# Rotary attention in a six-layer stage: each score step writes two single PSUM banks, and its exponential is done in two halves

## The reference, cut to what matters

```python
def _attn(q, k, v, mask):
    scores = jnp.einsum('bqhd,bkhd->bhqk', q, k) / np.float32(np.sqrt(HD))
    scores = jnp.where(mask[:, None, None, :], jnp.float32(-jnp.inf), scores)
    w = jax.nn.softmax(scores, axis=-1)
    return jnp.einsum('bhqk,bkhd->bqhd', w, v)
...
for i in range(NL):
    xn = _adaln(x, noise_emb, n1_w[i], n1_b[i])
    ...
    q = _rope(q.reshape(B, L, H, HD))
    k = _rope(k.reshape(B, L, H, HD))
    a = _attn(q, k, v, src_mask).reshape(B, L, D) @ so_w[i].T
    x = x + a
    ...
    a = _attn(q, k, v, ctx_mask).reshape(B, L, D) @ co_w[i].T
    x = x + a
    xn = _adaln(x, noise_emb, n3_w[i], n3_b[i])
    h = jax.nn.gelu(xn @ f1_w[i].T + f1_b[i], approximate=False)
    x = x + (h @ f2_w[i].T + f2_b[i])
```

## Time and profile before

| | |
|---|---|
| median of 3 runs | 4170.21 us (4165.55 to 4171.18) |
| the profiled execution | 4145.95 us, span of its instructions 4144.1 us |
| busy: TensorE, VectorE, ScalarE, GpSimd | 3599.2, 2465.0, 2296.2, 1355.3 us |
| stage 6 | from about 2269 us to the end, some 1875 us |
| mean granted TensorE clock | 0.949 of full speed |

### The profile page before, as it was taken

One profiled execution on the slowest core, in us unless ns is written; L12 is line 12 of the kernel. 1 busy time (PEld: TensorE's weight loads), 2 busy tenths in 40 slices (PEclk: granted clock), 3 DMA queues, 4 the chain that ended last, 5 costly groups with the idle time before them and its releaser, 6 DMA issues.

```text
span 4144.1 us, 56756 instructions
## 1 busy us (share of the span) xinstructions
PE 3599.2 (87%) x22327; PEld 1596.7 (39%) x22327; DVE 2465.0 (59%) x4758; ACT 2296.2 (55%) x3200; POOL 1355.3 (33%) x1355
## 2 busy tenths in 40 slices
PE   5699999899568988998895889898999998988886
PEld 4477433333443344334552233233333332333333
DVE  6732444544225345543658877777778677777754
ACT  4543554454124554545321766777767676776683
POOL 5500233333224511441003234344343442433411
PEclk8699999999799999999896999999999999999998
DMA  2000000000330010001111101111111110110100
GB/s 118 1 21 1 31 16 22 6 16 22 128 109 11 17 32 27 16 17 56 39 27 44 36 25 38 52 27 45 43 32 40 43 47 25 43 47 25 41 12 16
DMA packets 126956, 146.41 MB, mean 35 GB/s; under 512 B 36141, under 2 KB 107637, under 8 KB 124866
## 3 DMA queue, kind: packets, MB, share of 16 engines
q1 hardware_dynamic: 125664, 140.67, 11.5%
q0 software_dynamic: 1024, 2.10, 0.2%
HBM read 74.63 MB, written 6.43 MB: 20 GB/s over the span
## 4 chain that ended last, share of the span: by engine, by line
PE 59%; DVE 22%; ACT 8%; POOL 5%; DMA 3%; issue 3%; SPq 1%; POOLq 0%; DVEq 0%; ACTq 0%
PE ps L1903 6%; PE ps L1919 6%; PE ps L2114 6%; DVE c1sm L2862 4%; DVE c0sm L2862 4%; PE ps L2031 3%; PE ps L1823 3%; PE ps L1815 3%; PE ps L2100 3%; ACT wB L2358 2%; PE ps L2058 2%; PE ps L1951 2%; PE ps L1844 2%; PE ps L2158 2%; POOL c1m L3043 2%
## 5 line engine op out<-in xcount | busy, mean ns | idle before, releaser
L2358 ACT ACTIVATE wB<-ps 128x1024 f32<-128x1024 f32 (+1 forms) x762 | 762.1, 1022 | 270.0 <-PE ps L2100 263.8
L2862 DVE TENSOR_REDUCE c1sm<-ps 128x2 f32<-128x1024 f32 x384 | 456.6, 1220 | 128.1 <-PE ps L2058 125.3
L2862 DVE TENSOR_REDUCE c0sm<-ps 128x2 f32<-128x1024 f32 x384 | 453.2, 1219 | 97.2 <-PE ps L2058 95.3
L2656 DVE TENSOR_REDUCE c1sm<-ps 128x2 f32<-128x1024 f32 x128 | 151.7, 1220 | 194.0 <-PE ps L1868 192.8
L2656 DVE TENSOR_REDUCE c0sm<-ps 128x2 f32<-128x1024 f32 x128 | 152.5, 1221 | 172.3 <-PE ps L1868 171.3
L2358 ACT ACTIVATE c0m<-ps 128x1024 f32<-128x1024 f32 (+1 forms) x198 | 202.4, 1022 | 70.0 <-PE ps L2100 68.0
L2114 PE MATMUL ps<-wB,c1m 128*18 128x512 f32 (+1 forms) x1216 | 205.5, 611 | 1.1 <-DVE c1sm L2869 0.6
L1903 PE MATMUL ps<-c0ar 64*128 64x512 f32 (+1 forms) x640 | 178.1, 634 | 20.8 <-DVE c0sm L2656 9.1
L2100 PE MATMUL ps<-c0ar 64*128 64x512 bf16 (+1 forms) x864 | 167.0, 388 | 33.0 <-DVE c1sm L2862 14.4
L2100 PE MATMUL ps<-c1ar 64*128 64x512 bf16 (+1 forms) x864 | 165.3, 392 | 26.5 <-DVE c0sm L2862 9.2
L2992 POOL TENSOR_SCALAR c0sm<-c0sm 128x4 f32<-128x4 f32 x40 | 7.8, 194 | 547.9 <-DVE c0sm L2430 462.5
(11 more groups left out here) (918 smaller groups left out, 8268.1 us busy)
## 6 DMA issues: line engine op xcount, KB each, us to landing
c0ar<-c0m SPq DMA_DIRECT2D x216, 128.0 KB, 2.4
c1ar<-c0m SPq DMA_DIRECT2D x216, 128.0 KB, 2.4
c0m<-rscr SPq DMA_DIRECT2D x96, 128.0 KB, 2.9
c1m<-rscr SPq DMA_DIRECT2D x96, 128.0 KB
wA<-in_lay SPq DMA_DIRECT2D x6, 1346.0 KB, 5.6
c0ar<-in_x SPq DMA_DIRECT2D x15, 512.0 KB, 3.5
c1ar<-in_x SPq DMA_DIRECT2D x15, 512.0 KB
wA<-in_w SPq DMA_DIRECT2D x1, 4248.0 KB, 22.0
```

The source lines that it names most:

```text
L2358: e.activation(P.ap[0:n, :, :], u.ap[0:n, :].rearrange("p (a q) -> p a q", a=2), ACT.Exp, scale=S8).then_inc(*A(("P8", n0, s, k), free=[u]))
L2656: e.tensor_reduce(c.sm[:, 2 * (g % 2), 2 * j:2 * j + 2], u.ap.rearrange("p (h k) -> p h k", h=2)[:, :, 0:n], AX, ALU.max, negate=True).the ...
L2862: e.tensor_reduce(c.mneg[:, j, :, s // 4, s % 4], u.ap.rearrange("p (a k) -> p a k", a=2), AX, ALU.max, negate=True).then_inc(*V(free=[u]))
```

## The change

`s8` no longer takes a pair. It takes two single banks, which may lie in different pairs. Each of its two matmuls increments the semaphore. ScalarE does two exponentials of 512 columns instead of one of 1024, and each gives its bank back as soon as it is done. The planner is told 0.53 and 0.53 for the two halves instead of 1.03, and the kind of the chain is now `TAAb`, for which there is no bias. The waits for both banks stand ahead of the first matmul. Below this point the line numbers of the changed kernel are higher by one; the exponential stands in its line 2360, the matmuls of `s8` in line 2102.

```diff
-                        (u, P), t = yield Want([("T", .32), ("A", 1.03, "exp")], [two, P6], tm, True)
-                        emit("s8", c, l, n0, 2 * g + i, k, n, u, P, kkeys, cross)
-                        two.give(u, t[1])
-                        hold.append((P, t[1]))
+                        (u, u2, P), t = yield Want([("T", .32), ("A", .53, "exp"), ("A", .53, "exp")], [banks, banks, P6], tm, True)
+                        emit("s8", c, l, n0, 2 * g + i, k, n, (u, u2), P, kkeys, cross)
+                        banks.give(u, t[1])
+                        banks.give(u2, t[2])
+                        hold.append((P, t[2]))
...
-                for x in u.clear():
-                    w.wait_ge(*x)
+                for b in u:
+                    for x in b.clear():
+                        w.wait_ge(*x)
                 for p in range(2):
                     r = slice(64 * p, 64 * p + 64)
                     K = KC[l % 2][r, s, c.i, :] if cross else c.KS[r, s, 128 * k:128 * k + n]
-                    i = e.matmul(j4(u.ap, p, 512)[0:n, :], K, c.QS[r, s, :], start=True, stop=True)
-                i.then_inc(*T(("s8", n0, s, k)))
+                    e.matmul(u[p].ap[0:n, :], K, c.QS[r, s, :], start=True, stop=True).then_inc(*T(("s8", n0, s, k, p)))
                 T.mark(("s8", n0))
...
-                w.wait_ge(*T.at(("s8", n0, s, k)))
                 for x in P.clear():
                     w.wait_ge(*x)
-                e.activation(P.ap[0:n, :, :], u.ap[0:n, :].rearrange("p (a q) -> p a q", a=2), ACT.Exp, scale=S8
-                             ).then_inc(*A(("P8", n0, s, k), free=[u]))
+                for p in range(2):
+                    w.wait_ge(*T.at(("s8", n0, s, k, p)))
+                    e.activation(P.ap[0:n, p, :], u[p].ap[0:n, :], ACT.Exp, scale=S8).then_inc(*A(("P8", n0, s, k), free=[u[p]]))
```

## The result

The changed kernel takes 4209.53 us (median of 4 runs, 4206.78 to 4211.27), the kernel before 4167.88 us (4153.54 to 4171.18). The ratio is 1.0106, 95% interval 1.0081 to 1.0131: 1% slower, +42 us. The direction was forecast, and the time lies in the range, but the forecast was +14 us, and 4209.53 us is above the 4172 to 4205 us that went with it. The profiled executions are further apart (4211.27 against 4145.95, so 65 us), because the profiled run of before was its fastest. 11 of these 65 us lie ahead of the change: the first matmul that differs starts at 2268.83 us in one and at 2280.18 us in the other, after the same program.

The account below looks back on a forecast made before the run. No engine was taken as full in stage 6; TensorE leads its chain of waits, with coupling through PSUM. Terms +6 - 12 + 20 = +14 us gave 4184 us on the timed footing, range 4128 to 4245 us.

Parts of the forecast that it names:

- The split's term: Stage 6 exponentials: two of 512 columns cost 0.05 us more than one of 1024; +6 us, bounds 0 and +48.
- The share of 0.13: Worth at the end of a microsecond that ScalarE loses around the wB exponential: about 0.13.
- Where the banks come from: TensorE's bank waits in stage 6: `s8` and `m8` stop trading pairs; -12 us, bounds -48 us and nothing.
- What `m8` pays: 73 new handovers of pairs idle VectorE before `m8` reductions for 36 to 67 us; +20 us, bounds 0 and +67.
- What `s8` pays: ScalarE handovers to `s8` rise from 69 to 294, mostly covered by the second half; nothing, at most +13 us.
- The increment: Second semaphore increment on each `s8`: taken as 0; the Trainium skill's price would give up to 25 us.
- the last sentence on the numbers: The planner makes a new order for 1875 us of work; the terms count only what its bank waits show.
- decoupling wins: ScalarE and VectorE stop waiting for each other through pairs: -32 us, 4138 us; chance of the gain 0.31.
- pairs run out: Broken pairs starve `m8`: +60 us, 4230 us, at most +115; decided by reductions clearly above 14.3% of chain; chance 0.17.
- The clock leaves nothing to gain or lose: Clock granted at 0.98 to 1.00 in two stretches of stage 6, so nothing to gain or lose there.
- The signs that it named: Among others: `s8` waits for VectorE halve, idle before `m8` reductions grows 36 to 67 us, ScalarE busy up some 180 us.
- Two signs of being wrong: Among those named: exponentials above 5.4% of the chain; a stretch without PSUM waits moving more than a few us.

Follow-up runs that it names:

- banks given back together: Changed kernel, but both single banks are given back after the second half of the exponential, in program and plan: 4304.16 us, ratio 1.0352.
- the plan alone: Instructions of the kernel before, in the order the planner makes when told of two ScalarE pieces of .53: 4215.79 us, ratio 1.0139.
- another seed: Kernel before with another seed for the planner's small random term in stage 6, three tried: 4235.70, 4187.45 and 4228.13 us.
- the four differences: Changed form less form of before at four equal planner seeds, the own one and three others: +42, +40, +69 and -16 us.

## Why the prediction was right or wrong

- *Direction and range: right, in part by luck.* The sum was +14 us; measured +42. It is positive by the term for `m8`, which the runs don't bear out, and fresh orders of the same work scatter by more than the whole sum.
- *The split's term, +6 us: too small.* Alone it costs +16 us. The extra ScalarE time was nearly right (48 expected, 54 to 58 measured). The share of 0.13 was the error. It came from the exponentials' part of one chain. That part, as I read it now, is what an engine has on the path now, not what a longer instruction puts there: the same view of the split kernel gives 8.7%. I also took only the time to the next start (+0.05 us) and left out that each bank and each `P` comes 0.06 us later to those who wait for them.
- *Where the banks come from, -12 us: wrong sign.* The counts moved as read from the order, and `s8` behind VectorE gave up its time (37.0 to 6.2 us). But I priced each new wait like the old waits of its kind. `s8` behind wB went from 7.8/344 = 0.023 us to 42.0/757 = 0.055 us a wait. More of them are for the step right ahead, 294 of the 757 against 69 of the 344, which the prediction counted but did not price here. The net is +17 us of TensorE, or +24 us with the exponentials into `c0m`, whose time the term left out though its counts have them.
- *What `m8` pays, +20 us: not borne out.* The idle time rose by 13.5 us instead of 36 to 67 us, and the reductions' share of the chain fell. The kernel with the banks given back together shows that the mechanism exists. In the changed kernel it is small, 0.18 us for each of the 73 new handovers.
- *What `s8` pays, nothing:* right for ScalarE, whose idle time in front of exponentials fell by 24 us, which fits a second half that covers the handover. (Only 225 of the 294 such steps are new, so the 250 that can be covered are of all 294.) The cost came on TensorE, as the item on banks says.
- *The increment, 0: right.* At most 4 us of it reach the end.
- *What failed most* is the last sentence on the numbers, that the planner's new order is an uncertainty beside the terms. It is larger than any of them: +56 us for the plan alone, +20 to +70 us for another seed. What I can say of the +42 us is that a split costs 16 on the order of before. If that holds in the new order too, the other 26 are the order and the banks together. That an order alone can cost as much is shown; that the single banks cost nothing or gain is open, since the four differences scatter by more than their mean.
- *The rival "decoupling wins"* fails as a whole, but its mechanism is real in part: ScalarE idles less. *The rival "pairs run out"* is what the kernel with banks given back together looks like, at 4304 us: its late reductions have 17.3% of the stage's chain, more than the 14.3% that were to decide.
- *"The clock leaves nothing to gain or lose"* was wrong. It stood at 0.98 to 1.00 in the stretches that I read, and in the whole stage it fell from 0.98 to 0.96. I read it as a state of the kernel. Over the kernels run it moved with the order, and at the one place read in the changed kernel, gaps stood ahead of its fall; that the order's gaps cause it was not tried apart.
- *The signs that it named.* TensorE's waits for VectorE in front of `s8` fell by more than half, and VectorE's idle time grew, by less than forecast. Two signs of being wrong are there, both faint: the wB exponentials have 5.5% of the chain where they had 5.4, and the stage began 11 us later, which is no effect of the change, since the same program lies ahead of it. ScalarE's busy time was to go up by 180 us as shown; the page has 56 us. It counts overlapping instructions once. So the reading that TensorE's busy time counts some of it twice was wrong too: on the changed kernel's page, 768 `m8` matmuls of 0.404 us each (310 us in sum) are busy for 154.6 us.

## What to carry to other kernels

When a planner makes the order, the kernel before is one draw of it, and every edit of a cost or a buffer is a new draw. Before crediting a change with a per cent, redraw the unchanged kernel a few times; here that alone spanned 1.7%. To price the edit itself, put it into the old order: the split costs 0.4% there, and the increment nothing that can be measured. When two profiled executions are compared, start both at the same instruction: 11 of 65 us lay ahead of the change here.

Splitting an instruction on an engine that is a third idle still costs something: 0.06 us later each here, and 0.28 of it reached the end where the engine's share of the chain let expect 0.13.

## What the runs showed of the hardware

Two neighbouring 512-column exponentials from PSUM take 1.08 us together and 0.97 us to the next start, against 1.02 and 0.91 us for one of 1024. A second semaphore increment for each of 960 pairs of concurrent matmuls costs at most about 4 us in all. Eight of the `a8` matmuls took 1.05 us together at full clock and 1.89 us at half clock. In 31 executions of one program, a microsecond of clock not granted went with 0.56 us of time, and over the fourteen kernels the granted clock of the stage fell from 0.98 to 0.94 as it grew from 1872 to 2018 us.
